# Small pieces of work in other slots of an LSTM and feed-forward kernel, its last output sums cut by columns, and two quarters of x split on GpSimd

## The reference

```python
xW = jnp.einsum('ntd,dg->ntg', x, Wx) + b
def step(carry, xw_t):
    prev_h, prev_c = carry
    a = xw_t + prev_h @ Wh
    i, f, o = sigmoid(a[:, :Hd]), sigmoid(a[:, Hd:2*Hd]), sigmoid(a[:, 2*Hd:3*Hd])
    g = jnp.tanh(a[:, 3 * Hd:])
    next_c = f * prev_c + i * g
    next_h = o * jnp.tanh(next_c)
...
h = jnp.concatenate([h, -h], axis=-1)
h = jax.nn.relu(s0 * dense(k0, h)) * 2      # 512 -> 1024
h = jax.nn.relu(s1 * dense(k1, h)) * 2      # 1024 -> 1024
return x + s2 * dense(k2, h)                # 1024 -> 256
```

## Time and profile before

| what | us |
|---|---|
| three runs | 273.55, 274.23 (median), 274.58 |
| the profiled execution | 274.05 |
| its span | 272.3 |
| PE busy, DVE busy | 266.3, 220.0 |
| ACT busy, POOL busy | 187.2, 51.6 |
| steps, first to last h | 22.1 to 211.4 |

### The profile page before, as it was taken

One profiled execution on the slowest core, in us unless ns is written; L12 is line 12 of the kernel. 1 busy time (PEld: TensorE's weight loads), 2 busy tenths in 40 slices (PEclk: granted clock), 3 DMA queues, 4 the chain that ended last, 5 costly groups with the idle time before them and its releaser, 6 DMA issues.

```text
span 272.3 us, 8760 instructions
## 1 busy us (share of the span) xinstructions
PE 266.3 (98%) x3376; PEld 198.9 (73%) x3376; DVE 220.0 (81%) x847; ACT 187.2 (69%) x632; POOL 51.6 (19%) x68
## 2 busy tenths in 40 slices
PE   8999999999999999999999999999999999999995
PEld 5887877788889899999999998776655544444442
DVE  3778888898889989989899987886777799882474
ACT  5699888888867777766776766998876776223220
POOL 0100000011221122322123002131420373040120
PEclk9999999999999999999999999999999999999999
DMA  6980000000000000000010000000000010000004
GB/s 212 349 333 2 2 2 0 4 2 4 2 1 2 2 2 25 21 4 4 2 41 2 5 2 22 22 1 2 4 2 1 2 39 0 0 2 0 0 2 154
DMA packets 5145, 8.72 MB, mean 32 GB/s; under 512 B 624, under 2 KB 2672, under 8 KB 4976
## 3 DMA queue, kind: packets, MB, share of 16 engines
q1 hardware_dynamic: 4816, 7.64, 8.0%
q10 hardware_dynamic: 288, 0.52, 0.5%
HBM read 6.07 MB, written 2.10 MB: 30 GB/s over the span
## 4 chain that ended last, share of the span: by engine, by line
PE 79%; DVE 11%; ACT 5%; issue 2%; DMA 1%; DVEq 0%
PE WK L561 28%; PE WK L579 11%; PE G L523 9%; PE G L514 8%; PE WK L544 7%; PE G L579 5%; PE ACC L594 5%; PE WK L614 3%; DVE aT L980 2%; PE G L544 2%; ACT tT L719 2%; ACT tC L840 1%; PE ACC L614 1%; DMA x<-in_x 1%; PE G L614 1%
## 5 line engine op out<-in xcount | busy, mean ns | idle before, releaser
L561 PE MATMUL WK<-h,k 128*128 128x256 f16 (+1 forms) x696 | 92.6, 281 | 0.0
L561 PEld LDWEIGHTS WK<-h,k 128*128 128x128 fp8e5 x696 | 65.0, 98 | 11.3
L719 ACT ACTIVATE tT<-aT 128x64 f32<-128x64 f32 x189 | 44.3, 269 | 28.6 <-DVE aT L980 22.0
L980 DVE TENSOR_REDUCE aT<-G 128x64 f32<-128x128 f32 (+1 forms) x192 | 54.3, 331 | 9.1 <-PE G L523 8.9
L712 ACT ACTIVATE G<-xw 128x256 f32<-128x256 f32 x189 | 52.2, 297 | 0.0
L544 PE MATMUL WK<-xs,wxs 128*128 128x512 f32 x168 | 43.0, 401 | 0.0
L514 PEld LDWEIGHTS G<-h,w 128*128 128x128 f16 x1008 | 30.6, 96 | 12.6 <-DVE h L1094 9.8
L523 PE MATMUL G<-h,w 128*128 128x64 f16 x1008 | 39.5, 192 | 0.0
L514 PE MATMUL G<-h,w 128*128 128x32 f16 x1008 | 35.2, 177 | 1.0 <-DVE h L1094 0.7
L544 PEld LDWEIGHTS WK<-xs,wxs 128*128 128x128 f32 x168 | 30.4, 188 | 5.8
L523 PEld LDWEIGHTS G<-h,w 128*128 128x128 f16 x1008 | 33.2, 97 | 0.0
(11 more groups left out here) (126 smaller groups left out, 329.3 us busy)
## 6 DMA issues: line engine op xcount, KB each, us to landing
x<-in_x SPq DMA_DIRECT2D x3, 512.0 KB, 8.1
xw<-in_wh SPq DMA_DIRECT2D x4, 256.0 KB, 4.9
k<-in_k SPq DMA_DIRECT2D x1, 1024.0 KB, 10.1
out_y<-x SPq DMA_DIRECT2D x8, 128.0 KB, 1.8
out_y<-x SPq DMA_DIRECT2D x4, 256.0 KB, 2.0
x<-in_x ACTq DMA_DIRECT2D x2, 256.0 KB, 3.8
xw<-in_wx SPq DMA_DIRECT2D x4, 128.0 KB, 3.9
xw<-in_wx SPq DMA_DIRECT2D x2, 256.0 KB, 5.1
```

What stands on the lines that cost most here:

```text
L561: ins = eng.matmul(layer_src(tile), w, rhs, start=a == 0, stop=last)
L719: eng.activation(tT[:, B * j0:B * j1], aT[:, j0:j1].rearrange("p j b -> p (j b)"), ACT.Tanh, scale=half_gain0 if t == 0 else half_gain).th ...
L980: eng.tensor_reduce(aT[:, j0:j1], G[g][:, 0:64 * (j1 - j0)].rearrange("p (j h b) -> p j b h", h=2, b=B), op=ALU.add, axis=AX.X).then_inc(a ...
```

## The change

**P1's copy** moves from ScalarE to VectorE, and both it and c11_lo go by pieces: 128 columns in each of a step's two slots and the remaining 256 after h. Neither is done in full width any more, except the last two P2 tiles. The planner also keeps two chunk-4 tiles out of the same step on ScalarE, and a slot is open to any tile at the head of VectorE's list.

**Layer order:** tile (0, 1, 0) goes into the middle of (1, 0, 0).

**w1** is made in three pieces (768, 768 and 512 of 2048 columns) in steps 7, 8 and 9 instead of two of 1024.

**x:** GpSimd makes the high parts of quarter 2 before step 0 and those of quarter 3 in step 3, and the low parts of both in steps 0, 1, 4, 5; ScalarE and VectorE made them before.

**The end:** the second output half of chunk 4 is summed at the very end, first in 384 columns and then in 128, each with its own bank, y_add and DMA. `y_add` of chunk 3 stands behind the first block of terms instead of the second, and ACC is a bank like others.

```diff
-X2_STEPS = (1, 2)
+X2_STEPS = (0, 1)
 X3_STEPS = (4, 5)
+X3_HI_STEP = 3
 W0_STEPS = (0, 3, 6)
-W1_STEPS = (7, 8)
+W1_STEPS = (7, 8, 9)
+W1_ROWS = (0, 3, 6, 8)
...
-        at = (2, 2, 3, 4, 5, 6, 6, 7) if c == 0 else (0, 1, 2, 3, 4, 5, 6, 6) if c < N1 - 1 else (3, 4, 5, 6, 7, 7)
+        at = (8, 2, 3, 4, 5, 6, 6, 7) if c == 0 else (0, 1, 2, 3, 4, 5, 6, 6) if c < N1 - 1 else (3, 4, 5, 6, 7, 7)
...
-            if m < 2 and c:
+            if m == 0 and c == 0:
+                order += [((1, 0, 0), 12), ((0, 1, 0), 4), ((1, 0, 0), 4)]
+            elif m < 2 and c:
...
-    order += outs(N1, 0, 1, 2, 3)
+    order += [(("o", N1, k), part) for k in range(4) for part in range(2)]
...
-    order += outs(N2, 0, 1) + products(6, 2, 3) + outs(N2, 4, 5) + products(7, 2, 3) + outs(N1, 4, 5) + products(4, 2, 3)
-    order += outs(N2, 2, 3, 6, 7)
-    return order + [(("o", N1, k), 2 * mo + part) for mo in range(2) for k in (6, 7) for part in range(2)]
+    order += outs(N2, 0, 1) + products(6, 2, 3) + outs(N2, 4, 5) + products(7, 2, 3)
+    order += [(("o", N1, k), part) for k in (4, 5) for part in range(2)] + products(4, 2, 3)
+    order += outs(N2, 2, 3, 6, 7) + [(("o", N1, k), part) for k in (6, 7) for part in range(2)]
+    return order + [(("o", N1, k), 2 * piece + part) for piece in (1, 2) for k in range(8) for part in range(2)]
...
-        between[t] = [x for x in todo[:1] if x[0] in (0, 1)]
-        todo = todo[len(between[t]):]
+        between[t] = todo[:1]
+        todo = [x for x in todo if x not in between[t] or x[0] in ("p1", "p2")]
...
+            if tile[:2] == (0, N1) and any(x[:2] == (0, N1) for x in act[t]):
+                held.append((tile, 0.0))
+                emptied.discard(tile)
+                chores.remove(tile)
+                continue
+            if tile[0] != "p1":
+                act[t].append(tile)
             if tile not in emptied:
-                (late if spent - at < 0.75 else todo).append(tile)
+                (late if spent - at < 0.75 or tile[0] in ("p1", "p2") else todo).append(tile)
...
-            now = todo[:1 if len(todo) + len(late) < 4 or t in W2_STEPS else 2]
+            now = todo[:1 if len(todo) + len(late) < 4 or t in W2_STEPS or todo[0][0] in ("p1", "p2") else 2]
...
+            def product_part(tile, cols, last):
+                if tile[0] == "p1":
+                    p1_copy(tile, cols, last)
+                else:
+                    c11_lo(tile, cols, last)
+
             def half_lo(tile, half):
 
+                if tile[0] in ("p1", "p2"):
+                    product_part(tile, slice(128 * half, 128 * half + 128), False)
+                    return
                 cols = slice(width(tile) // 2 * half, width(tile) // 2 * (half + 1))
...
+            def p1_copy(tile, cols, last):
+                e.wait_ge(prod_mm[1], tile[1] + 1)
+                e.wait_ge(seeded[O], 40)
+                ins = eng.tensor_copy(p1s[:, tile[1], cols], layer_src(tile)[:, cols])
+                if last:
+                    ins.then_inc(p1_made)
...
-                if k == 1:
+                if k == 0:
                     for mo in range(2):
                         y_add(N1 - 1, mo)
...
+            def x_hi(i, k):
+                eng.wait_ge(dx[i - 1], 16)
+                if i > 1:
+                    eng.wait_ge(x_mm, NJ * (i - 1))
+                eng.tensor_copy(xs[:, i % 2, 0, k, :], x[:, k, 512 * i:512 * i + 512]).then_inc(xh_late)
+
             for k in range(2):
-                eng.tensor_copy(xs[:, 1, 0, k, :], x[:, k, 512:1024]).then_inc(xh1)
+                x_hi(1, k)
+            eng.wait_ge(hz_lo, 1)
+            for k in range(2):
+                x_hi(2, k)
+
+            def x_lo(i, k):
+                eng.wait_ge(xh_late, 2 * (i - 1) + k + 1)
+                eng.tensor_tensor(xs[:, i % 2, 1, k, :], x[:, k, 512 * i:512 * i + 512], xs[:, i % 2, 0, k, :].bitcast(F32),
+                                  ALU.subtract).then_inc(xl_late)
...
+                if t in X2_STEPS:
+                    x_lo(2, X2_STEPS.index(t))
+                if t in X3_STEPS:
+                    x_lo(3, X3_STEPS.index(t))
+                if t == X3_HI_STEP:
+                    for k in range(2):
+                        x_hi(3, k)
```

120 lines of the change are left out of this document (58 added, 62 removed).

## The result

| | us |
|---|---|
| kernel before, beside it (4 runs) | 273.89 median (273.39 to 274.58) |
| changed kernel (4 runs) | 276.64 median (274.79 to 277.34) |
| ratio | 1.0087, 95% interval 1.0067 to 1.0106 |
| changed kernel, 6 later runs beside 23 of before | 275.30 against 273.82: 1.0054 (1.0034 to 1.0074) |
| profiled execution of the changed kernel | 274.79, span 272.7 |

The change made the kernel slower, by 0.5% to 0.9%; the forecast was 272.6 and its range ended at 273.9. Three of the first four executions had a mean granted TensorE clock of 0.993 to 0.994, the profiled one of 1.000. So two things have to be found: what kept the profiled execution from the 1.4 us that were forecast, and what happens in the others.

The account below looks back on a forecast made before the run. TensorE's order and its few waits were taken to set the time, with VectorE's chain close beside. Steps 1.7 us less and the end 0.3 more gave 274.05 - 1.7 + 0.3 = 272.65, stated as 272.6; range 271.7 to 273.9.

Parts of the forecast that it names:

- interval 18, layer order: Stretch between h of steps 17 and 18: fewer layer matmuls in step 17 bring 3.17 to 2.94, 0.23 us less.
- intervals 8 and 9, w1: Stretches ending at h of steps 8 and 9: shorter w1 pieces on VectorE remove most excess over 2.94, 0.34 us less.
- interval 4: Stretch between h of steps 3 and 4: ScalarE's copy goes, but GpSimd's CASTs behind w0 hold uT; 0.12 us less.
- interval 1, first subtraction beside w0: Stretch between h of steps 0 and 1: GpSimd's subtraction may wait for w0 and delay uT; 0.2 us more.
- interval 2, x on GpSimd: Stretch between h of steps 1 and 2: VectorE's gain and the wait on GpSimd cancel, 0.
- end: After step 63: output work moved last leaves TensorE idle 1.8 us ahead of P7; smaller last pieces compensate; 0.3 us more.
- What GpSimd gets instead starts 0.7 after h: Early steps: GpSimd's x work starts 0.7 us after h, so a 1.30 us subtraction is over at 2.0.
- the slow rival: Intervals 1, 2, 4, 5, 6: GpSimd's float32 work holds the reduces too; 4 us more, 276.4; 0.05 together with the clock.
- a held instruction starts at 1.87, which is where uT starts anyway: Intervals 2, 5 and 6: uT, held by GpSimd's subtraction, starts at 1.87 after h as in interval 1; net 0.
- TensorE's granted clock falls in the new idle time: Ahead of P7: the clock drops, the 32 us behind take up to twice as long; 0.05 together with the slower case.
- "no lock" rival: Intervals 1, 2, 4, 5, 6: 64-column instructions aren't held, 0.6 us more gained, last DMA gives 0.6; 271.9; chance 0.07.
- The saved waits come back in part: Interval 1, one of intervals 56, 61, 63, and the end lose 0.9 us in all, giving 273.5; chance 0.22.

Follow-up runs that it names:

- b_lock: Kernel before plus five unread GpSimd subtractions of 512 columns, one each in intervals 43, 45, 47 and two in 51: 276.49 us, ratio 1.0096.
- e_best: Changed kernel with c12 sums earlier, x's third-quarter low parts on VectorE (step 1) and GpSimd (step 2), and the old layer order: 271.44 us, ratio 0.9914.
- e_late: Changed kernel with VectorE's first two c12 sums earlier and GpSimd's x low parts in steps 2, 3, 5, 6, fourth-quarter high parts in 4: 271.99 us.
- e_x2: Changed kernel with GpSimd's two subtractions for x's third quarter in steps 1 and 2 instead of 0 and 1: 274.04 us.
- e_nox: Changed kernel with x's third and fourth quarter split on ScalarE and VectorE again, as before: 273.63 us, ratio 0.9988.
- e_stall: Changed kernel with two more unread 512-column GpSimd subtractions between the two of x's third quarter: 278.48 us, ratio 1.0168.
- e_dve: Changed kernel with VectorE's first two c12 sums moved ahead of the low parts of the fourth term: 273.68 us.
- e_oldend: Changed kernel with the old order of the end, the two 512-column output halves and the old place of chunk 3's sum: 275.27 us.
- b_x: Kernel before with only the change's x work on GpSimd: 276.27 us, ratio 1.0084.
- e_lib: Changed kernel with VectorE's earlier c12 sums and a four-column GpSimd subtraction of zeros behind the CASTs of x's second quarter: 273.23 us.
- b_stall: Kernel before with three back-to-back GpSimd subtractions in interval 45, starting 1.9 to 2.0 behind h: 276.51 us, ratio 1.0109.
- b_dve: Kernel before with only VectorE's first two c12 sums moved ahead of the fourth term's low parts: 273.83 us, ratio 0.9999.

## Why the prediction was wrong

| step of the prediction | forecast | measured (profiled executions) |
|---|---|---|
| interval 56, P1's copies off ScalarE | -0.53 | -0.54 |
| interval 59 | -0.13 | -0.15 |
| intervals 61 and 63, pieces | -0.65 | -0.66 |
| slots (interval 60) | +0.1 | +0.11 |
| interval 18, layer order | -0.23 | -0.22, but 17 +0.12 and 19 +0.16 |
| intervals 8 and 9, w1 | -0.34 | -0.16 |
| interval 4 | -0.12 | -0.27 |
| interval 3 | 0 | -0.09 |
| intervals 5 to 7 | 0 | +0.13 |
| interval 1, first subtraction beside w0 | +0.2 | 0, it wasn't there |
| **interval 2, x on GpSimd** | **0** | **+1.25** |
| end | +0.3 | +0.5 |
| start, up to the first h (varies by 1.1 from trace to trace) | 0 | +0.3 |
| device time outside the span | 0 | +0.3 |
| in other executions: the clock | 0 | +1.0 to +2.6 |

**The step that failed** is "What GpSimd gets instead starts 0.7 after h". It was read from rows 4, where GpSimd's instructions are in the middle of their work. The first two subtractions are the first TENSOR_TENSOR behind an instruction of another kind (the reduction over the partitions, L1170), and the first of them starts 6.7 to 8.3 us behind GpSimd's last CAST, whatever it waits for: 6.72, 7.21, 7.16, 7.16, 6.73, 7.14, 7.30 and 6.98 in eight traces and, for four columns of zeros, 8.33 us. So both came in interval 2 at 0.99 behind h and not at 0.7 in two intervals. The trace of before has the same pair of MODIFY_POOL_CONFIG at 14.3, and its first use of it (L1155) at 53.7, so no row there shows the wait. The Trainium skill (GPSIMD Engine Reference, section "2.1 Instruction dispatch") says that the first call to a freshly loaded kernel of GpSimd pays a load of about 6 us that the profile doesn't show as an instruction. The traces agree in kind, with 6.7 to 8.3 us. An estimate by the page's 6 us, from the pair at 20.1, puts the first subtraction at 26.1 for an h at 25.79, so in interval 2 with the second behind it. That the wait is a load of code no run here shows; they show when it comes and how long it is.

**What it does to VectorE** I had right in kind. An instruction with both operands in SBUF doesn't run beside GpSimd's, one that reads PSUM does: the reduces in interval 2 of the changed kernel start 1.01 behind h and take 0.86, so the slow rival (the reduces stand) is out in its own form. My sum "a held instruction starts at 1.87, which is where uT starts anyway" holds for a subtraction at 0.7: `b_lock`'s interval 43 costs 0.00. It doesn't hold for one that starts 0.3 to 1.3 later: then it covers uT or vT, and each 0.1 of it counts (0.46 for a start at 1.23, 0.94 at 1.8, 1.07 at 2.0), and two in a row cost 1.25 to 2.0. `e_best` and `e_late`, without a late subtraction, have interval 2 at 3.01 and 2.93. I gave the term no bound from that side, because I took the start as known.

**The clock.** I had named it as a rival, at the wrong place: "TensorE's granted clock falls in the new idle time" ahead of P7. That idle time (1.38) brings no fall: 12 executions of `e_x2` and 12 of `e_nox` have it, all at 1.000. The low clock goes with the wait in interval 2 (theory B of the first runs, C of `e_stall`). Of 36 executions with two late subtractions (the changed kernel, `e_dve`, `e_oldend`, `b_x`; intervals 2 of 4.26 to 5.03 in their profiles) 11 have a clock of 0.992 to 0.994; of 60 executions of the other kernels up to `b_lock`, and of those of the kernel before, none is below 0.998. `e_stall` makes the wait longer, and all four fall. Within one of the later kernels a low clock costs 1.0 us (`b_x`, medians 276.73 against 275.71) to 1.8 (`e_oldend`, 277.02 against 275.18); the changed kernel's first runs had it in three of four, hence their 276.6. In none of those executions was the fall itself recorded in a profile; that it lies in interval 2 there is inferred from `e_stall`. What decides it isn't settled. TensorE's idle time in interval 2 of those profiles is 1.09 to 1.86, which includes the 1.38 ahead of P7 and the 1.39 in interval 1 of `e_lib`, where 31 executions in all show no fall; 2.64 gave one of four (`b_stall`), 3.48 four of four. So the place may count beside the length, or the executions that fell had a longer wait than the profiled ones.

**Smaller errors.** The w1 pieces bring 0.16 and not 0.34, since TensorE has 3.05 of its own work in intervals 5 to 9 (nine matmuls of x and the gates; busy 3.05 of 3.05 in the row of 45.13). I had compared with intervals of 2.94 that hold other matmuls. The same bound gives intervals 5 to 7 their 0.04 each: the plan has nine there in both kernels, but before, TensorE was still ahead of h and lost 0.04 of that lead per step. Interval 4 was better than thought: GpSimd's CASTs didn't start behind w0's step but beside it (0.7 to 2.1 behind h, 1.42 for the two instead of 1.18) and left uT at 1.88. In interval 19 h comes 0.54 behind the start of tanh of c instead of 0.26 to 0.3. The length of this pause of VectorE differs from kernel to kernel in the same interval (0 in `b_x`, 0.1 before, 0.26 after, 0.36 in `e_nox`, there ahead of cD), and `e_best` has it with the layer order of the kernel before; its cause stays open.

**The end was nearly right.** P7 forecast at 237.2, measured 237.21, though its idle time is 1.38 by the modelled ends instead of 1.8. TensorE's end comes 1.33 later from the last h (58.93 against 57.60; forecast 1.27), and the time between it and the end of the span is 0.87 shorter (forecast 0.9). What I had too small is the delay of the c12 sum: 0.15 forecast, 0.30 measured behind the last h. Its reason isn't the term that I named but TensorE, which leaves the shortened intervals 0.32 later behind h (`e_oldend`). This is the rest of the end's +0.47. `e_dve` confirms why the end brings nothing: with the c12 sums ahead TensorE doesn't wait at P7, and the stretch behind the last h is 59.8, 1.5 less than with the new order alone and 1.1 less than before, while the sums alone (`b_dve`) bring nothing.

**And the "no lock" rival**, 271.9, is out by `b_lock`. "The saved waits come back in part" was right for 17, 19 and 60 (0.4 together) and for the 0.3 behind the last h, but apart from the end it named other places, and would have given 273.5.

What remains unexplained is 0.3 us in `e_nox`: its trace is 0.7 shorter than before at an equal start, its median 0.2, and 0.2 more lies outside the span. The start before the first h varies by more than the rest, and 12 runs don't settle it. Open as well is why the device time exceeds the span by 2.0 to 2.2 in the changed kernel and most of its variants, by 1.8 in the kernel before and all of its variants, `b_x` among them, and by 1.9 in `e_best`.

## What to carry to other kernels

Before an engine's work is moved to GpSimd, look in its records for when that kind of instruction was last used: the first one behind a change of kind came 6.7 to 8.3 us behind the one before it here, and a first user that the chain waits for pays it. A two-operand GpSimd instruction beside VectorE costs what is left of it when VectorE's next instruction with both operands in SBUF is due, from nothing to about its whole length here (0 to 1.07 of 1.28 us); so its place is a start time, not a step. And a change that moves work off TensorE's wait to the end is worth it only if what TensorE then waits for is moved ahead as well: six instructions of VectorE in another order were worth 1.6 us here, and nothing without the change. A saved wait ahead of a stretch in which TensorE has no gap comes back there: 0.32 of interval 63's 0.33.

## What the hardware showed that I had not expected

- The wait for GpSimd's first TENSOR_TENSOR grew from 6.7 to 7.3 us to 8.33 where it fell into the last loads from HBM (14.2 to 22.5 us), though its waits were all met. One run shows it; that the loads are the reason wasn't tried.
- One TENSOR_SCALAR of 64 columns with a single tile operand in SBUF (oP, L1088) stood for 1.27 us beside the third subtraction of `b_stall`, like those with two. GpSimd's CAST, with one operand, let w0's TENSOR_TENSOR stand until it ended: 1.11 instead of 0.68 in `e_lib`. It goes the other way too: w0's step held GpSimd's CASTs (1.42 instead of 1.18) and its subtraction (1.52 instead of 1.28).
- A fall of the clock costs 2.3 us in `e_stall`, more than a whole subtraction, and follows a wait of 3.48 us of TensorE; a wait of 2.64 (`b_stall`) went with a low clock in one execution of four.
